# A selective-scan tower: decays in SBUF two groups deep, carries beside each segment, new orders on all engines

## What is computed

```python
def selective_scan(u, dt, Bm, Cm, A, Dp):
    def step(h, inp):
        u_t, dt_t, B_t, C_t = inp
        dA = jnp.exp(dt_t[..., None] * A)
        h = h * dA + (dt_t * u_t)[..., None] * B_t[:, None, :]
        y = jnp.einsum('bdn,bn->bd', h, C_t)
        return (h, y)
    ...
    return jnp.swapaxes(ys, 0, 1) + u * Dp

def mamba(u, in_w, conv_w, conv_b, xproj_w, dt_w, dt_b, A_log, Dp, out_w):
    x, z = jnp.split(u @ in_w.T, 2, axis=-1)
    x = silu(dwconv_causal(x, conv_w, conv_b))
    x_dbl = x @ xproj_w.T
    dt = jax.nn.softplus(x_dbl[..., :R] @ dt_w.T + dt_b)
    Bm, Cm = x_dbl[..., R:R + N], x_dbl[..., R + N:]
    y = selective_scan(x, dt, Bm, Cm, -jnp.exp(A_log), Dp)
    return y * silu(z) @ out_w.T
```

## Time and profile before

| | |
|---|---|
| median of 3 runs | 552.32 us (547.97 to 553.13) |
| the profiled execution | 551.16 us, of which the core's span is 549.3 us |
| granted PE clock, mean over the span | 0.935 of full |
| busy: PE, DVE, ACT, POOL | 465.3, 483.8, 373.3, 478.5 us |
| first scan on DVE, last instruction of POOL | 46.15 us, 523.8 us |

### The profile page before, as it was taken

One profiled execution on the slowest core, in us unless ns is written; L12 is line 12 of the kernel. 1 busy time (PEld: TensorE's weight loads), 2 busy tenths in 40 slices (PEclk: granted clock), 3 DMA queues, 4 the chain that ended last, 5 costly groups with the idle time before them and its releaser, 6 DMA issues.

```text
span 549.3 us, 5677 instructions
## 1 busy us (share of the span) xinstructions
PE 465.3 (85%) x1659; PEld 181.0 (33%) x1659; DVE 483.8 (88%) x602; ACT 373.3 (68%) x656; POOL 478.5 (87%) x153
## 2 busy tenths in 40 slices
PE   6896886979799797979898889888997887795987
PEld 2432322323233232424233424343333332332333
DVE  3679879779898999999999999998899999999951
ACT  2475877476867777786968687858776885374633
POOL 5773889978979989899999999999999999999810
PEclk9897999889979898989999989979899998796999
DMA  5468641765071724426172717181717171700000
GB/s 60 27 48 236 209 155 40 249 217 157 32 242 38 234 78 150 162 93 218 62 231 83 239 63 248 54 253 54 252 50 253 58 253 48 256 16 10 0 11 19
DMA packets 50256, 70.79 MB, mean 129 GB/s; under 512 B 15874, under 2 KB 16818, under 8 KB 50226
## 3 DMA queue, kind: packets, MB, share of 16 engines
q1 hardware_dynamic: 47954, 69.20, 38.5%
q0 software_dynamic: 1024, 1.05, 3.3%
q10 hardware_dynamic: 1248, 0.19, 0.2%
HBM read 58.36 MB, written 9.96 MB: 124 GB/s over the span
## 4 chain that ended last, share of the span: by engine, by line
PE 36%; DVE 32%; issue 15%; ACT 8%; POOL 8%; DMA 0%; DVEq 0%; ACTq 0%; POOLq 0%
DVE st L1600 16%; DVE st L1585 6%; PE ps L638 6%; POOL st L506 5%; PE ps L731 3%; PE ps L719 3%; POOL st L497 2%; ACT ps L1114 2%; PE ps L813 2%; PE ps L549 2%; PE ps L699 2%; PE ps L681 2%; PE ps L829 2%; PE ps L612 2%; PE ps L665 2%
## 5 line engine op out<-in xcount | busy, mean ns | idle before, releaser
L506 POOL TENSOR_TENSOR st<-st,repC 128x2048 f32<-128x2048 f32 x63 | 285.9, 4547 | 21.0 <-ACT carry L1120 13.6
L1600 DVE TENSOR_TENSOR_SCAN st<-ps,carry,st 128x512 f32<-128x512 f32 x192 | 235.2, 1267 | 10.9 <-ACT ps L1114 10.3
L1114 ACT ACTIVATE ps<-dtS,negA 128x512 f32<-128x512 f32 x256 | 170.9, 682 | 47.2 <-DVE st L1600 43.9
L497 POOL TENSOR_TENSOR st<-duS,repB 128x2048 f32<-128x2048 f32 x31 | 141.0, 4548 | 2.0 <-PE ps L719 2.0
L1600 DVE TENSOR_TENSOR_SCAN st<-ps,zero,st 128x512 f32<-128x512 f32 x64 | 78.9, 1269 | 5.8 <-ACT ps L1114 5.4
L719 PE MATMUL ps<-st,fold 128*32 128x512 f32 x504 | 70.4, 625 | 15.4 <-POOL st L506 15.4
L1585 DVE TENSOR_TENSOR st<-duS,ps 128x2048 f32<-128x2048 f32 x32 | 72.7, 2271 | 0.2 <-PE ps L699 0.2
L638 PE MATMUL ps<-act,wT 128*128 128x512 f32 x128 | 57.7, 593 | 0.0
L470 POOL DMA_INDIRECT x<-in_L_tok_ple_table,idx x32 | 31.2, 976 | 12.5 <-issue 9.1
L681 PE MATMUL ps<-xr,wT 128*32 128x512 f32 x32 | 19.6, 697 | 22.5 <-DVE st L1585 22.5
L813 PE MATMUL ps<-xfT,w 97*128 97x512 f32 x64 | 35.2, 642 | 1.3 <-ACT xfT L1139 0.7
(11 more groups left out here) (150 smaller groups left out, 633.1 us busy)
## 6 DMA issues: line engine op xcount, KB each, us to landing
repC<-bc_dram SPq DMA_DIRECT2D x64, 256.0 KB, 4.8
duS<-du_dram SPq DMA_DIRECT2D x60, 256.0 KB, 3.3
dtS<-dt_dram SPq DMA_DIRECT2D x60, 256.0 KB, 4.2
repB<-bc_dram SPq DMA_DIRECT2D x31, 256.0 KB, 3.0
dt_dram<-dt SPq DMA_DIRECT2D x15, 256.0 KB, 3.2
du_dram<-du SPq DMA_DIRECT2D x15, 256.0 KB, 2.0
bc_dram<-bc_sb SPq DMA_DIRECT2D x16, 64.0 KB, 4.7
dtS<-dt SPq DMA_DIRECT2D x4, 256.0 KB, 5.7
```

The source lines that it names most:

```text
L497: pool.tensor_tensor(st[:, r], duS[:, u % 2], row, ALU.mult).then_inc(sem("dbu_pool"), 1)
L506: pool.tensor_tensor(st[:, r], st[:, r], row, ALU.mult).then_inc(sem("hc_ready"), 1)
L1114: sc.activation(decay_bank(u, r, q), dtS[:, u % 2, q], ACT.Exp, scale=negA[:, way(u), q, r:r + 1]).then_inc(sem("decay_ready"), 1)
L1600: dve.tensor_tensor_scan(st[:, r, q, order], decay_bank(u, r, q)[:, order], st[:, r, q, order], first, ALU.mult, ALU.add).then_inc(sem("sc ...
```

## The change

Nothing of the arithmetic changes. What changes is where things lie and in what order the lists stand.

- `dec`, a new SBUF tile of two groups, takes the decays. The PSUM banks 0, 1 and 2 are free of them and become `ROWS` (B's rows for DVE), `BC` and `ZED`; the norm's scratch gets bank `STAT` to itself. ACT makes the four decays of a group in a row, when the group two before has been scanned.
- Each segment of `st` and `dec` gets a column beside it: a group is now W = 4 x 513 + 1 columns wide. The column of `dec` is 0, the column of `st` holds the carried state, so a scan runs over 513 columns and starts from `zero`. `keep_last` copies the segments' last columns into those beside (and, where a direction starts anew, writes zeros), so it runs in every unit but the last: 60 small copies where there were 48.
- A scan is still one instruction for each segment, and waits for its own decay.
- The lists of DVE and ACT are now written by groups (`between(u, r)`), so that a group's four scans stand in a row; PE's and SP's lists are reordered around the new banks. C's rows are loaded group by group into six buffers; `xr` has three buffers, not four, `zr` two.
- POOL makes its input product of unit 0 ahead of dt times x of unit 1.
- The sum of squares of the norms of units 12 to 14 is on DVE (both inputs `xc` in SBUF), not on ACT.

```diff
+    W = NQ * (T + 1) + 1
-        st = sb("st", [P, NR, NQ, T])
+        st = sb("st", [P, NR, W])
+        dec = sb("dec", [P, 2, W])
-        def decay_bank(u, r, q):
-            return ps[:, (NQ * NR * u + NQ * r + q) % 3, :]
+        def segment(q):
+            return slice((T + 1) * q + 1, (T + 1) * q + 1 + T)
+        def columns(r):
+            return st[:, r, 1:W].rearrange("p (q t) -> p q t", t=T + 1)[:, :, 0:T]
+        PADS = slice(0, W, T + 1)
+        def scanned_cols_of(ap, u, q):
+            at = (T + 1) * q
+            return ap[:, at + 1:at + T + 2][:, ::-1] if way(u) else ap[:, at:at + T + 1]
...
             def decay(u, r, q):
-                wait(sc, "scanned", scan_nth(u, r, q) - 3)
-                sc.activation(decay_bank(u, r, q), dtS[:, u % 2, q], ACT.Exp,
+                if q == 0:
+                    wait(sc, "scanned", scan_nth(u, r) - 2)
+                sc.activation(dec[:, r % 2, segment(q)], dtS[:, u % 2, q], ACT.Exp,
                               scale=negA[:, way(u), q, r:r + 1]).then_inc(sem("decay_ready"), 1)
...
             def keep_last(u, r):
-                    sc.activation(carry[:, r, :], st[:, r, :, 0 if way(u) else T - 1], ACT.Copy) \
+                if not carries(u):
+                    mm = sc.activation(st[:, r, PADS], zero[:], ACT.Copy)
+                elif way(u):
+                    mm = sc.activation(behind[:, :, T], behind[:, :, 0], ACT.Copy)
+                else:
+                    mm = sc.activation(ahead[:, :, 0], ahead[:, :, T], ACT.Copy)
...
             def by_c(u, r):
-                pool.tensor_tensor(st[:, r], st[:, r], row, ALU.mult).then_inc(sem("hc_ready"), 1)
+                pool.tensor_tensor(columns(r), columns(r), row, ALU.mult).then_inc(sem("hc_ready"), 1)
...
-                dve.tensor_tensor_scan(st[:, r, q, order], decay_bank(u, r, q)[:, order], st[:, r, q, order],
-                                       first, ALU.mult, ALU.add).then_inc(sem("scanned"), 1)
+            def scan(u, r):
+                scan_all(u, r)
+                for q in range(NQ):
+                    dve.wait_ge(sem("decay_ready"), NQ * (scan_nth(u, r) - 1) + q + 1)
+                    scan_part(u, r, q, "scanned" if q == NQ - 1 else "part_scanned")
+            def scan_part(u, r, q, name):
+                cols = scanned_cols_of(st[:, r], u, q)
+                dve.tensor_tensor_scan(cols, scanned_cols_of(dec[:, r % 2], u, q), cols, zero[:, 0:1],
+                                       ALU.mult, ALU.add).then_inc(sem(name), 1)
...
+            input_product(0, 2)
+            dt_times_x(1)
             for u in range(UNITS):
                 if u:
                     by_c(u - 1, NR - 1)
-                if u == 0:
-                    dt_times_x(1)
-                if 2 in on_pool(u):
                     input_product(u, 2)
```

More of the change, by code:

```diff
@@ L190, in build @@
         repB = sb("repB", [P, 2, 2, T])
-        repC = sb("repC", [P, 2, NR, T])
+        repC = sb("repC", [P, 6, T])
         v_ = sb("v_", [P, T])
@@ L423, in _ @@
             load_B(0)
-            load_C(0)
+            for r in range(NR):
+                load_C(0, r)
             store_bc(1)
@@ L909, in _ @@
[L909 to L918 removed]
+                if ended:
+                    turn_normed(ENDS[u - 1])
+                if settled:
+                    hidden(ENDS[u - 2], 3)
@@ L938, in _ @@
[L938 to L947 removed]
+                if quick:
+                    hidden(u - 2, 2)
+                    hidden(u - 2, 3)
@@ L948, in _ @@
+                if settled:
+                    experts_out(ENDS[u - 2])
+                if u - 1 not in QUICK:
+                    partial(u - 1)
+                if ended:
+                    turn_choice(ENDS[u - 1])
+                if u == 1:
+                    zed(2)
+                    gate_chunk(3, LONG)
+                if u == QUICK[0]:
+                    for v in zeds(u):
+                        zed(v)
                 if 2 <= u <= CB + 1:
                     gate_chunk(CB + u - 2, LONG)
-                if is_unit(u):
-                    sum_states(u, 1)
@@ L1360, in _ @@
-            for p in range(NR * NQ):
-                decay(0, p // NQ, p % NQ)
-                first_unit(p)
+            sc.wait_ge(sem("rows_ready"), 1)
+            decay(0, 0, 0)
+            softplus_exp(1)
+            decay(0, 0, 1)
+            softplus_plus1(1)
+            softplus_ln(1)
+            decay(0, 0, 2)
+            bc_out(1)
+            decay(0, 0, 3)
+            uT_chunk(2)
+            decays(0, 1)
+            uT_chunk(3, ZED)
+            dt_out(1)
+            keep_last(0, 0)
@@ L1363, in _ @@
+            decays(0, 2)
+            silu_tables()
+            act_silu(2, LONG)
+            act_silu(3, ZED)
+            z_silu(0)
+            z_silu(1)
+            conv_silu(2, PRE)
+            keep_last(0, 1)
+            exp_ln_tables()
+            decays(0, 3)
+            keep_last(0, 2)
+            decays(1, 0)
+            softplus(2)
+            bc_out(2)
             for u in range(1, UNITS):
-                for p in range(NR * NQ):
-                    decay(u, p // NQ, p % NQ)
-                    between(u, p)
+                for r in range(NR):
+                    keep_last(*((u, r - 1) if r else (u - 1, NR - 1)))
+                    decays(*((u, r + 1) if r < NR - 1 else (u + 1, 0)))
+                    between(u, r)
@@ L1761, in _ @@
-            for p in range(NR * NQ):
-                if p < NQ:
-                    first_product(p)
-                scan(0, p // NQ, p % NQ)
-                first_unit(p)
-            for u in range(1, UNITS):
-                for p in range(NR * NQ):
-                    scan(u, p // NQ, p % NQ)
-                    between(u, p)
-            last, before = UNITS - 1, UNITS - 2
-            dve.wait_ge(sem("scanned"), scan_nth(last, NR - 1, NQ - 1))
-            dve.wait_ge(sem(f"repC_in_{last % 2}"), 64 * (last // 2 + 1))
@@ new lines, in _ @@
+            log1p_error(1)
+            first_product(3)
+            first_scan(3)
+            input_product(0, 1)
+            scan(0, 1)
+            start_residual(2)
+            scan(0, 2)
+            input_product(0, 3)
+            start_residual(3)
+            scan(0, 3)
+            last, before = UNITS - 1, UNITS - 2
+            for u in range(1, UNITS):
+                for r in range(NR):
+                    if (u, r) == (last, NR - 1):
+                        scan_all(u, r)
+                        dve.wait_ge(sem("decay_ready"), NQ * scan_nth(u, r))
+                        for q in range(NQ):
+                            scan_part(u, r, q, "last_scanned")
+                    else:
+                        scan(u, r)
+                    between(u, r)
```

708 lines of the change are left out of this document (307 added, 401 removed).

## The result

The changed kernel takes 826.02 us (median of 4 runs, 823.89 to 828.11) against 551.99 before (the three runs of the table above and a fourth): a ratio of 1.498, 95% interval 1.491 to 1.505. The profiled execution took 828.11 us, its span is 826.3. Some executions of the kernel before and of its near variants are 1 to 2% longer than the rest (555.69 to 559.31 us in 4 of 17, at a granted PE clock of 0.914 to 0.920, against 546.79 to 554.98 in the others), and all ratios leave such executions out.

What follows compares the result with a forecast made beforehand. DVE and POOL, both full, bound the kernel side by side. Taking turns: first scan 46.15 + scans 314.1 + products 450.1 + tail 25.5 = 835.9, corrected by 24 + 4 - 13 to 851, plus 1.86 outside: 853 us, range 590 to 905.

Steps and rivals of the forecast that it cites:

- The central step: Scans reading dec and st never run beside POOL's products, so their stretch is the sum, 314.1 + 450.1 us; chance 0.62.
- The gathers' excess: Three POOL gathers of the kernel before, normally 0.94 us, ran 0.21 to 0.37 us longer beside two-SBUF-input DVE instructions.
- The direction that one row left open: Whether a DVE instruction waits for a running POOL product; one row fitted a wait or a sharing by halves.
- The 0.12 us of L1773: DVE's L1773, near the program's end, lost 0.12 of the 0.25 us it ran beside POOL's last product.
- The first rival: Partial contention: POOL stands for a running scan, scans beside a product lose only 0.12 us; 610 us, chance 0.19.
- POOL's products, 450.1 us: Sum of POOL's products; the gaps between segments were taken to add 0, at most 0.52 us a product.
- Idle and overlap, 24 + 4 - 13 = +15: Corrections: 24 us for carry copies between turns, 4 for the first four scans, less 13 for product starts beside scans.
- The tail, 25.5 us: Time behind POOL's last product, taken unchanged from the kernel before.
- DVE's other work hidden: DVE's 169.7 us besides scans read at most one SBUF tensor and would hide beside POOL's products.
- PE's clock: PE, idle more, gets a lower granted clock; up to 3 us a unit allowed, 48 us, only in the upper bound.
- Two groups deep: Decay buffering that can remove ACT's 43.9 us and DVE's 15.7 us of waits; worth nothing under turn-taking.
- The second rival: No contention: POOL alone bounds, and half of its 23.2 us idle time is won; 540 us, chance 0.19.

Runs made afterwards that it cites:

- sbuf_decays_alone: Kernel before with only its three decay buffers moved from PSUM to SBUF; 843.47 us, ratio 1.531.
- padded_st_only: Kernel before with only st laid out in steps of 513 columns, decays still in PSUM; 545.45 us, ratio 0.9885.
- one_scan_per_group: Kernel after with the four scans of each of 62 groups merged into one; 772.08 us, ratio 1.402.
- pool_writes_only: Kernel after with POOL's input products and products with C replaced by pairs of memsets; 573.67 us, ratio 1.041.
- one_input_by_c: Kernel after with POOL's product with C replaced by a product with a constant, reading one tensor; 792.22 us, ratio 1.433.
- one_decay_in_four_sbuf: Kernel before with the decays of each group's first segment in SBUF, the others in PSUM; 636.5 us, ratio 1.150.

## Why the prediction held, point by point

**The central step** was right: that scans which read dec and st never run beside POOL's products, so that the stretch becomes the sum of both. The gathers' excess of 0.21 to 0.37 us, on which it stood, pointed the right way, and sbuf_decays_alone shows that this part alone makes it. That a product of 4.5 us would behave as the gathers did was not in those rows, and there is some luck in it: L1515, also with two SBUF inputs, ran from 37.23 to 37.92 beside the gather of 36.70 to 38.01 and kept its 0.69 us, so a gather seems to stand only at one point near its start. A product with two inputs holds scans off to its end. The Trainium skill (SBUF — State Buffer, § Who interferes with whom) says that a DVE instruction with two SBUF inputs contends with a GpSimd instruction that reads SBUF, not with one that only writes it. The traces agree in both halves: 5.5 us for the longest scan beside reading products, 1.26 us for the median beside memsets. Its "for the whole instruction" is too much for the one-input product, which let go 1.74 us before its end.

**The direction that one row left open**, a scan behind a running product, was a wait to the end: 1.08 us from the product's end to the scan's. The 0.12 us of L1773 was not half a wait but a short one: it ended 0.56 us after POOL's last product (523.77). The same instruction in sbuf_decays_alone met that product earlier, stood 0.82 us beside it, and again ended 0.55 us after it. Rows from the timelines of DVE and POOL:

```profile
814.73 1.37 DVE L1774 TENSOR_TENSOR st<-st,repC 128x512 f32<-128x512 f32 x1
...
813.38 2.17 POOL L534 TENSOR_TENSOR st<-st,repC 128x512 f32<-128x512 f32 x1
```

The first rival (610 us) read the row of the kernel before wrongly.

**The size** was 27 us too high, 853 for 826 (for the profiled execution 853 for 828.1). That it came within 3% is in part luck: the terms were off by 24, 11 and 9 us, not all to the same side, and the range of 590 to 905 would have held a much larger miss. The terms, by the trace of after:

- POOL's products, 450.1 us: the mis-sized term. I took the gap at 0, with 0 to +0.52 us a product as bounds. It was -0.37 us for the 63 products with C, 24 us in all. My reason for 0 was that C's and B's rows were read four times over before too, and nothing in it excluded a shorter product; padded_st_only shows that the layout alone makes it so.
- Idle and overlap, 24 + 4 - 13 = +15: neither a scan nor a product was in flight for 37 us for my 28, but what passes while an instruction stands is more than my 13. Of the 37 us, 52 short gaps of at most 0.51 us, nearly all behind a group, make 17.5 (my 24), and ten longer ones make 19.8. The longest, 4.77 us at 148.8, ends with a carry copy that stood behind ACT's silus and table loads; the prediction had said that the unit's rhythm would cover this. With the other terms taken from the trace (first scan at 47.6, scans 314, products 426, tail 34.6, sum 822) the overlap comes to 33 us, so the net is +4.
- The tail, 25.5 us: it was 34.6, from 791.7 to 826.3. The 9 us are PE's clock: PE is busy 16.39 us for 7.45 in the stretch below. The tail up to the last transpose of `xf` takes 18.7 us at a granted clock of 0.50, the lower level, where the same work took 9.8 us at 1.00; what follows takes 15.8 for 15.7. Columns as in the earlier trace rows, the kernel after, then before:

```profile
791.70:810.40 18.70, 16.39 (x38) 7.23 (x39) 6.41 (x19) 3.99 (x9) 0.00 (x0) 0.50 0.04 8
...
523.80:533.60 9.80, 7.45 (x32) 3.58 (x32) 6.00 (x17) 2.97 (x7) 0.00 (x0) 1.00 0.06 15
```

  In the 10 us ahead of it PE was busy 4.72 us at 0.50 in the kernel after, and 9.52 us at 1.00 in the kernel before. It comes with the new lists and not with the decays in SBUF: one_scan_per_group, pool_writes_only and one_input_by_c have the same stretch at 0.50 to 0.52 and tails of 34 us, sbuf_decays_alone and one_decay_in_four_sbuf, with the old lists, at 1.00 and 25 us. Which piece of the lists does it, no run tells.
- DVE's other work hidden: only in the main. No wait of POOL's in the profile ends with it, but DVE was at it for 28 of the 37 us in which neither a scan nor a product was in flight. Most of that lay beside the carry copies and cost nothing of its own; at 106.4 us its input product and `log1p_error` filled a gap of 2.7 us that ended with a scan. The three sums of squares moved to DVE took 1.85, 1.85 and 1.58 us for 0.42, since products held them.
- PE's clock: right in kind (0.77 mean for 0.935), and the 3 us a unit that I allowed upwards were not needed. It cost 9 us where I had put nothing, in the tail.

**Two groups deep** was worth nothing, as forecast: ACT still waits for DVE, 129.9, 101.3 and 52.3 us before its carry copies, and DVE waits 1.7 us for decays.

**The second rival** (540 us, no contention) comes nearest in pool_writes_only, and even there the time was 574. It seems to have overrated the new lists: half of POOL's idle time was to be won, and in that run they lose 21 us, 8 of them in the tail.

## What to carry to other kernels

Where VectorE and GpSimd are both full, count for every VectorE instruction how many of its inputs lie in SBUF. The second one made it take turns with GpSimd's products, which read SBUF, and the two lists added up: here one line that moved three buffers from PSUM to SBUF cost 53%. One such instruction among others is not cheap either, since it pays up to a whole GpSimd instruction (4.2 us for a scan of 1.26).

A short overlap at the edge of a trace can decide such a question: three gathers that were 0.2 to 0.4 us too long, each by the rest of another engine's instruction less 0.12 us, told more than all the busy shares. Such a row says that two instructions exclude each other, but not for which part of them. And when a change loses, take its harmless parts one at a time: the padding alone is a gain of 1.2%.

## What the runs showed of the hardware that was not expected

- A GpSimd product of 4 x 512 float32 columns takes 4.55 us when the segments of its st or duS input touch, and 4.18 us with a gap of 1 column between them (for st of 8 columns too).
- The same 2048 columns times a constant take 5.37 us on GpSimd, longer than times a second tensor (4.17); a memset of them takes 1.81.
- A product that reads one tensor holds VectorE's two-input instructions off for its first 3.6 of 5.4 us; one that reads two, to its end.
- A held scan of 512 or 513 columns ends 1.08 to 1.09 us after the end of a two-input product in the four runs that have both (kernel after, sbuf_decays_alone, one_decay_in_four_sbuf, one_input_by_c); free, it takes 1.26 us.
- With the lists of the kernel after, PE's granted clock is at its lower level for the first 18 us of the tail, even in a run of 574 us (0.52), and that costs 8 to 9 us.
